# A mixture-of-experts kernel: each token's row is stored once in SBUF and carries both experts' data, and SyncE's copies of the normalized rows are taken out

## The reference

```python
x = x + elu(softmax(mask(leaky(e_src + e_dst))) @ Wh)      # of layernorm(x), Wh = layernorm(x) @ W
n = layernorm(x)
scores, idx = top_k(n @ Wg.T + bg, 2)                       # 2 of 8 experts
p = softmax(scores)                                         # p1 = 1/(1+exp(gap)), p2 = exp(gap)*p1
for e in range(8):
    y = relu(n @ W1[e].T + b1[e]) @ W2[e].T + b2[e]         # 128 -> 512 -> 128
    out = out + combine[..., e] * y                         # combine is p1, p2 or 0
x = x + out
```

## Time and profile before

| | |
|---|---|
| median of 3 runs | 451.71 us (451.34 to 453.06) |
| profiled execution, its span | 546.0 us (one execution; no other time of it is given) |
| engine busy, share of the span | TensorE 81%, VectorE 66%, ScalarE 58%, GpSimd 53% |
| attention steps, 60 to 246 us | TensorE 126.93 us busy, GpSimd 90.72 |
| steady expert blocks, 320 to 480 us | TensorE 159.91 us busy |
| SyncE's 32 copies into rows | 256 KB each |

### The profile page before, as it was taken

One profiled execution on the slowest core, in us unless ns is written; L12 is line 12 of the kernel. 1 busy time (PEld: TensorE's weight loads), 2 busy tenths in 40 slices (PEclk: granted clock), 3 DMA queues, 4 the chain that ended last, 5 costly groups with the idle time before them and its releaser, 6 DMA issues.

```text
span 546.0 us, 9056 instructions
## 1 busy us (share of the span) xinstructions
PE 443.0 (81%) x2246; PEld 330.6 (61%) x2246; DVE 362.3 (66%) x1410; ACT 318.7 (58%) x760; POOL 288.2 (53%) x292
## 2 busy tenths in 40 slices
PE   7796777665686776657998499999999999998990
PEld 3564555554464554545765388777778787886740
DVE  6576576566566664656786278678777777767754
ACT  2675466454555665547475397777777776757700
POOL 1206554444565544355467456655566565664662
PEclk8988887787888877777799799999999999999996
DMA  6982221122222211323324123332332323247789
GB/s 189 316 335 79 77 68 59 46 69 74 78 73 79 73 57 43 88 78 117 88 72 154 57 63 87 103 98 74 92 102 82 99 77 97 77 144 226 233 258 333
DMA packets 56291, 63.03 MB, mean 115 GB/s; under 512 B 7744, under 2 KB 40896, under 8 KB 56000
## 3 DMA queue, kind: packets, MB, share of 16 engines
q1 hardware_dynamic: 35728, 33.28, 20.6%
q0 software_dynamic: 9344, 20.10, 11.0%
q10 hardware_dynamic: 11184, 9.26, 5.6%
HBM read 27.28 MB, written 26.94 MB: 99 GB/s over the span
## 4 chain that ended last, share of the span: by engine, by line
PE 57%; another core or an unknown queue 13%; ACT 11%; issue 8%; DVE 6%; DMA 2%; SPq 2%; ACTq 1%; DVEq 0%; POOL 0%; POOLq 0%
PE bank L1438 6%; PE bank L1422 6%; PE bank L1435 6%; PE bank L1426 5%; PE bank L1436 5%; PE bank L1423 5%; PE bank L1323 5%; PE bank L1382 4%; ACT prob L595 4%; PE bank L1384 3%; PE bank L1304 2%; PE bank L1414 2%; PE bank L1406 2%; ACT xn L635 1%
## 5 line engine op out<-in xcount | busy, mean ns | idle before, releaser
L508 POOL DMA_INDIRECT expert_slots<-rows,slot_i x128 | 126.7, 990 | 132.4 <-DVE slot_i L872 94.7
L1323 PE MATMUL bank<-wh,prob_t 128*128 128x128 f32 x128 | 29.2, 400 | 51.4 <-ACT prob_t L603 45.1
L1435 PE MATMUL bank<-hh,w_hi 128*128 128x512 f32 x144 | 62.2, 432 | 5.7 <-DVE hh L1136 3.1
L700 ACT ACTIVATE yb<-bank,b_sb 128x512 f32<-128x512 f32 x36 | 24.8, 690 | 66.4 <-PE bank L1438 43.1
L1422 PE MATMUL bank<-xh,w_hi 128*128 128x512 f32 x144 | 60.6, 421 | 0.8 <-ACT xh L685 0.8
L1438 PE MATMUL bank<-hl,w_hi 128*128 128x512 f32 x144 | 59.6, 414 | 0.1
L1423 PE MATMUL bank<-xh,w_lo 128*128 128x512 f32 x144 | 58.6, 407 | 0.0
L1436 PE MATMUL bank<-hh,w_lo 128*128 128x512 f32 x144 | 58.4, 406 | 0.0
L1323 PEld LDWEIGHTS bank<-wh,prob_t 128*128 128x128 f32 x128 | 25.0, 291 | 55.0 <-ACT prob_t L603 47.9
L1426 PE MATMUL bank<-xl,w_hi 128*128 128x512 f32 x144 | 58.3, 405 | 0.0
L524 POOL DMA_INDIRECT moe_rows<-hrelu,ysi x40 | 41.4, 1035 | 30.5 <-issue 15.1
(11 more groups left out here) (166 smaller groups left out, 1108.8 us busy)
## 6 DMA issues: line engine op xcount, KB each, us to landing
rows<-xn SPq DMA_DIRECT2D x32, 256.0 KB
xs<-expert_slots SPq DMA_DIRECT2D x27, 260.0 KB
x_all<-x SPq DMA_DIRECT2D x16, 256.0 KB, 3.8
w_raw<-w_t SPq DMA_DIRECT2D x2, 2048.0 KB, 13.6
w_raw<-moe_rows SPq DMA_DIRECT2D x16, 256.0 KB, 4.1
out<-x_all ACTq DMA_DIRECT2D x16, 256.0 KB
xs<-expert_slots ACTq DMA_DIRECT2D x11, 260.0 KB
w_hi<-moe_rows SPq DMA_DIRECT2D x9, 256.0 KB, 4.6
```

Of the source, the lines that this page charges most:

```text
L508: nc.gpsimd.indirect_dma_start(out=slots, out_offset=bass.IndirectOffsetOnAxis(ap=slot_i[q][:, k * SUB + j:k * SUB + j + 1], axis=0), in_= ...
L700: nc.scalar.activation(yb[:, :], ps_y[:, :], ACT.Identity, bias=b2_sb[:, e:e + 1]).then_inc(yb_ok, 1)
L1323: last = nc.tensor.matmul(tiles(ps_av)[:, j, :], prob_t[:, j, :], wh[:, j, :], start=True, stop=True)
L1435: nc.tensor.matmul(ps_y[:, :], w2_hi[:, e, c, :], hh[:, c, :], start=c == 0, stop=False)
```

## The change

A token's row is now stored in SBUF once, in a ring of three buffers `rows[n]` (`RING`, group mod 3). ScalarE's second norm writes the features there directly, TensorE turns them from there, and GpSimd's eight DMAs of a group send the same four rows twice. SyncE's copies and the buffers `xn2` are gone. A row has 133 numbers: 128 features; `PICK`, two numbers, the difference of the first choice's weight and output number against the second's; `SECOND`, two numbers, the second choice's own; and `TOP`, the number of the expert that was chosen first. TOP is written by a new ScalarE copy (`top_rows`) behind the second norm, and GpSimd waits for it (`top_row_ok`) and for `xn2_ok` in place of `rowx_ok`. When a block is loaded, `keep_meta` picks: (TOP equals this block's expert) x PICK + SECOND. The block's expert comes from a table `expert_of` of 72 entries that VectorE computes once, from the block bounds and 72 new columns of constants. Output numbers are kept as float32.

```diff
-WEIGHT, ID = D, D + 1
-ROW = D + 2
+PICK, SECOND, TOP = D, D + 2, D + 4
+ROW = D + 5
+RING = 3
...
-        xn2 = [sb(f"xn2_{q}", [P, SUB, D]) for q in range(2)]
-        rows = [sb(f"rows{q}", [P, 2, SUB, ROW]) for q in range(2)]
+        rows = [sb(f"rows{n}", [P, SUB, ROW]) for n in range(RING)]
...
-                for k in range(2):
-                    sp.dma_start(rows[q][:, k, :, 0:D], xn2[q][:, :, :]).then_inc(rowx_ok, 16)
...
+            rows_sent(sp, SURE_GROUPS)
             load_block(sp, sure_row(0), 0)
...
                     pool.wait_ge(slot_ok, gr + 1)
-                    pool.wait_ge(rowx_ok, 32 * (gr + 1))
...
+                    pool.wait_ge(xn2_ok, SUB * (gr + 1))
+                    pool.wait_ge(top_row_ok, gr + 1)
...
-                                in_=rows[q][:, k, j, :], in_offset=None).then_inc(rows_out[q], 16)
+                                in_=rows[gr % RING][:, j, :], in_offset=None).then_inc(rows_out[gr % RING], 16)
...
+            def top_rows(gl):
+
+                act.wait_ge(topf_ok, gl + 1)
+                nc.scalar.copy(rows[gl % RING][:, :, TOP], top_f[:, 0, :]).then_inc(top_row_ok, 1)
...
-                if later(gx - 1):
-                    act.wait_ge(rowx_ok, 32 * (gx - 1))
+                if gx >= RING:
+                    act.wait_ge(rows_out[gx % RING], 16 * 2 * SUB * (gx // RING))
...
+            def weight_gap(gl):
+
+                dve.wait_ge(p2_ok, gl + 1)
+                nc.vector.tensor_tensor(rows[gl % RING][:, :, PICK], first_p[:, :], rows[gl % RING][:, :, SECOND], ALU.subtract)
...
-                nc.vector.tensor_copy(meta[:, bass.ds(i & (META - 1), 1), :, :].rearrange("p n t k -> p (n t) k"),
-                                      xs[:, :, WEIGHT:ROW]).then_inc(meta_ok, 1)
+                if not isinstance(i, int) or i > 0:
+                    dve.wait_ge(meta_ok, i + FIRST)
+                nc.vector.scalar_tensor_tensor(picked[:, :, :], xs[:, :, TOP:ROW].to_broadcast([P, SUB, 2]),
+                                               expert_of[:, bass.ds(i, 1)], xs[:, :, PICK:SECOND], ALU.is_equal, ALU.mult
+                                               ).then_inc(picked_ok, 1)
+                dve.wait_ge(picked_ok, i + 1)
+                nc.vector.tensor_tensor(meta[:, bass.ds(i & (META - 1), 1), :, :].rearrange("p n t k -> p (n t) k"),
+                                        picked[:, :, :], xs[:, :, SECOND:TOP], ALU.add).then_inc(meta_ok, 1)
...
+            nc.vector.tensor_tensor(reached[:, :, :], cst[:, C_BLOCK:C_END][:, :, None].to_broadcast([P, BLOCK_NOS, E]),
+                                    until_f[:, None, :].to_broadcast([P, BLOCK_NOS, E]), ALU.is_ge).then_inc(late_ok, 1)
+            dve.wait_ge(late_ok, 1)
+            nc.vector.tensor_reduce(expert_of[:, SURE_BLOCKS:], reached[:, SURE_BLOCKS:, :], AX, ALU.add).then_inc(late_ok, 1)
```

More of the change, by code:

```diff
@@ L44 @@
 STAGES = 5
+BLOCK_NOS = 72
 MASKED = -1e30
@@ L59 @@
 C_FULL = C_PAD + SUB
-C_END = C_FULL + FULL
+C_BLOCK = C_FULL + FULL
+C_END = C_BLOCK + BLOCK_NOS
 def shape_constants(np):
@@ L335, in gnn_moe_kernel @@
         x_in = [sem(f"x_in{n}") for n in range(LOADS)]
-        rows_out = [sem(f"rows_out{q}") for q in range(2)]
+        rows_out = [sem(f"rows_out{n}") for n in range(RING)]
         scattered = [sem(f"scattered{b}") for b in range(BUFS)]
@@ L340, in tiles, with rows_sent @@
             return ap[:, :].rearrange("p (t j) -> p t j", t=SUB)
+        def rows_sent(eng, groups):
+            for n in range(RING):
+                eng.wait_ge(rows_out[n], 16 * 2 * SUB * len(range(n, groups, RING)))
         def later(n):
@@ L422, in _ @@
             sp.dma_start(b2_sb[:, :], b2_t).then_inc(c_b2, 16)
[L424 to L434, removed]
-                for k in range(2):
-                    sp.dma_start(rows[q][:, k, :, 0:D], xn2[q][:, :, :]).then_inc(rowx_ok, 16)
[L438 to L443, removed]
+            rows_sent(sp, SURE_GROUPS)
             load_block(sp, sure_row(0), 0)
-            pass_on(SURE_GROUPS // 2 + 1, 1)
-            for q in range(2):
-                pass_on(GROUPS // 2 - 1, q)
             sp.wait_ge(table_ok, 1)
             bounds = [SURE_BLOCKS]
-            for q in range(2):
-                sp.wait_ge(rows_out[q], 16 * 2 * SUB * (GROUPS // 2))
+            rows_sent(sp, GROUPS)
             n = sp.value_load(count_i[0:1, E - 1:E], min_val=0, max_val=TOKENS)
@@ L672, in step @@
                 if gx is not None:
-                    second_norm(gx, q)
+                    second_norm(gx)
+                if gl is not None:
+                    top_rows(gl)
                 if g0 is not None:
@@ L712, in drain @@
                 elu_exp(last)
-                second_norm(last - 1, 0)
-                act.wait_ge(rows_out[0], 16 * 2 * SUB * (SURE_GROUPS // 2 + 1))
-                act.wait_ge(rows_out[1], 16 * 2 * SUB * (SURE_GROUPS // 2))
+                second_norm(last - 1)
+                top_rows(last - 2)
+                rows_sent(act, SURE_GROUPS)
                 load_block(act, sure_row(1), 1)
@@ L727, in drain @@
                 load_block(act, sure_row(2), 2)
-                second_norm(last, 1)
+                top_rows(last - 1)
+                second_norm(last)
                 turned_norm(last)
@@ L733, in drain @@
                 gap_exp(last)
+                top_rows(last)
                 hidden(1, 0, 2)
@@ L868, in write_slots @@
                 dve.wait_ge(slotp_ok, gr + 1)
-                if later(m - 2):
-                    dve.wait_ge(rows_out[q], 16 * 2 * SUB * (m - 2))
+                if gr >= 2:
+                    dve.wait_ge(rows_out[(gr - 2) % RING], 16 * 2 * SUB * ((gr - 2) // RING + 1))
                 with nc.allow_low_precision(reason="one term of a sum is a slot's number, the others are zero"):
@@ L1091, in step @@
                 if gl is not None:
-                    row_ids(gl, q)
+                    weight_gap(gl)
+                    row_ids(gl)
                 if isinstance(t, int) and t + 1 < len(BATCHES):
@@ L1192, in drain @@
                 gap_sum(last - 1)
-                first_weight(last - 1, q, m)
-                second_weight(last - 1, q)
-                row_ids(last - 1, q)
+                first_weight(last - 1)
+                second_weight(last - 1)
+                weight_gap(last - 1)
+                row_ids(last - 1)
                 halve(0, 2)
@@ L1213, in drain @@
                 weigh(0, 0, 0)
-                first_weight(last, 1 - q, (t + 1) // 2)
-                second_weight(last, 1 - q)
-                row_ids(last, 1 - q)
+                first_weight(last)
+                second_weight(last)
+                weight_gap(last)
+                row_ids(last)
                 write_slots(last, q, (t + 1) // 2)
@@ L1337, in rank, with norm_turns @@
                 last.then_inc(rank_ps, 1)
-            def norm_turns(gx, q):
+            def norm_turns(gx):
                 for j in range(SUB):
                     pe.wait_ge(xn2_ok, SUB * gx + (j + 1))
-                    last = nc.tensor.transpose(tiles(ps_t3)[:, j, :], xn2[q][:, j, :], ident)
+                    last = nc.tensor.transpose(tiles(ps_t3)[:, j, :], rows[gx % RING][:, j, 0:D], ident)
                 last.then_inc(xn2_ps, 1)
@@ L1463, in drain @@
                 pe.wait_ge(xn2_t_ok, last - 1)
-                norm_turns(last - 1, 0)
+                norm_turns(last - 1)
                 hidden(0, 0, 2)
@@ L1473, in drain @@
                 result(0, 0, 1)
-                norm_turns(last, 1)
+                norm_turns(last)
                 result(0, 0, 2)
```

71 lines of the change are left out of this document (38 added, 33 removed).

## The result

| | kernel before | changed kernel |
|---|---|---|
| median | 451.52 us (451.13 to 453.06, 4 runs) | 456.33 us (455.80 to 457.55, 4 runs) |
| ratio | 1 | 1.0114, 95% interval 1.0086 to 1.0143 |
| profiled span | 546.0 us | 454.7 us |

The changed kernel is 4.8 us (1.1%) slower. The forecast was 453.5, with 446 to 458 as the range: the sign and the range held, but the sum of 1.75 us was too small by a factor of 2.7. The median also lies above the 451.5 to 455.5 that the prediction gave to its own case D, near the times of the rivals B (457.2) and C (457.0).

What follows compares the result with a forecast made beforehand. TensorE was read as busiest (81%) and full in the expert blocks; in the attention steps a ring of work, no engine near full. Terms 0.3 + 1.0 + 0.3 + 0.15 = 1.75 us slower gave 453.5 us; range 446 to 458.

Steps and rivals of the forecast that it cites:

- case D: Whole kernel: the forecast itself, 451.5 to 455.5 us; chance 0.44.
- Rival B: Attention steps: GpSimd's start, 3.7 us later per group, is passed on; 457.2 us at most; chance 0.18.
- Rival C: Expert blocks: keep_meta costs in most blocks, half of 36, 4.5 us instead of 1.0; 457.0 us; chance 0.14.
- drain: Between attention and experts: three of the new ScalarE copies fall there, 0.1 each, 0.3 us.
- I take four such places: Expert blocks: keep_meta's second operation, some 0.25 us, shows in four places; 1.0 us, bounds 0 and 9.0.
- Together 3.0 us against 1.86 of idleness plus 0.9 of TensorE's lead: VectorE behind block 3: the table's 1.6 us plus 1.4 already there, mostly hidden; 0.3 us exposed, bounds 0 and 1.6.
- It cannot be in the measured time to that extent: Attention steps: the profiled stalls after SyncE's copies are mostly absent from runs; 94.3 us belong to the profiled execution alone.
- I take nothing: Attention steps: the copies' stalls in the measured time, between nothing and some 25 us, are put at 0.
- if the copies cause the stalls: Sign in the new profile: span falls to some 470 to 500 us, prob_t no longer waiting for an unknown releaser.
- 10.0 us a step, an estimate: Attention steps: unprofiled length of one of 11.7 steps, after taking 69.5 us of waits off 186 us.
- GpSimd's 10.2 us is a floor: Attention steps: GpSimd's eight scattered stores, 10.2 us a group, limit the step even if all stalls are removed.
- Rival A: Attention steps: part of the stalls is real and 6 us go, so the kernel is faster, 447.5 us; chance 0.24.

Runs made afterwards that it cites:

- e3: Kernel before with keep_meta as two dependent copies in place of one in each block; 453.49 us, ratio 1.0025.
- e7: Changed kernel with keep_meta's sum moved behind hl of chunk 0 and a smaller, later table over 42 blocks; 452.68 us, ratio 1.0023.
- e9: Changed kernel with only keep_meta's sum moved behind hl of chunk 0, table as it was; 453.17 us, ratio 1.0077.
- e5: Kernel before with the table of experts alone added, including its 72 columns of constants; 451.43 us, ratio 0.9999.
- e1: Changed kernel with ScalarE's copy of the expert number placed right behind the exponential of the gap, so GpSimd starts earlier; 456.03 us, ratio 1.0095.
- e4: Kernel before with only the step's additions: ScalarE's copy, GpSimd's wait for it, one more VectorE subtraction; 451.19 us, ratio 1.0011.
- c0: Kernel before, unchanged, profiled a second time; span 451.0 us, and the run took 452.85 us.
- e6: Kernel before with 7 + 3 filler matmuls, results unused, in the drain; 448.76 us, ratio 0.9938.
- e2: Changed kernel with 7 + 3 filler matmuls, results unused, in the drain; 452.52 us, ratio 1.0051.
- e8: Kernel before with one unused tile of 32 bytes per partition ahead of xs, no instruction changed; 449.20 us, ratio 0.9982.

## Why the prediction held, and which terms were mis-sized

The forecast's mechanism was right in the main: the removed copies were hidden, and most of the rise that can be assigned is VectorE's new work in the expert blocks. Its size was not: every term that showed was put too low, and the time stayed in the range because the range was wide. The terms, beside what they measured:

| term | put at | measured |
|---|---|---|
| keep_meta | 4 places x 0.25 = 1.0 | 8 places x 0.24 = 1.9 (e3; gone in e7, e9) |
| table | 0.3 | 1.0 in the changed kernel, 0.65 in e5 |
| drain | 0.3 | up to 0.9, from profiles that scatter by 0.6; 0.1 with fillers |
| steps, ring, GpSimd, SyncE | 0 | 0.2 (e1 and e4: none that can be told) |
| constants | 0.15 | not seen; the fourth z copy starts at 40.4 to 43.5 us, whatever the kernel |
| addresses of tiles | not thought of | steady blocks 6.43 for 6.46: -0.6 |

These add up to +3.4 us. The runs say +4.8 (3.9 to 6.5) for the changed kernel and +4.3 (3.0 to 5.6) for e1. So 0.9 to 1.7 us (by the ratio 5.1 for the changed kernel) are not assigned, and up to 0.9 more if the drain is no part of the loss.

- **"I take four such places".** This is the step that failed most. The price of a place was right (0.25 against 0.24 in the mean); the count was an estimate. The earlier trace rows were taken in a steady block, and the places that matter were within the reach of the same trace: every change of expert, eight of them.
- **"Together 3.0 us against 1.86 of idleness plus 0.9 of TensorE's lead".** The 1.86 us come from a steady block too. Behind block 3 VectorE also makes the low halves of the weights and has no idle time. The duration of 1.6 us was nearly right (0.78 + 0.72), the cover was not.
- **The drain.** The three ScalarE copies were priced by their length. The time that can be won in the drain lies elsewhere, in short gaps on TensorE after which its clock is at half, and both kernels have them. That the new operations lengthen these gaps is not shown.
- **"It cannot be in the measured time to that extent" and "I take nothing".** Right: 94.3 us belonged to that one execution. The first followed from the two times; the second was a choice between 0 and 25 us, made with numbers of the odd profile, and there luck helped. What I said would show the cause was worthless, though. The new profile's span did fall below 500 us with prob_t waiting no longer, just as "if the copies cause the stalls" demanded, and the copies did not cause them: c0 has them and spans 451.0. A comparison with one profile of each kernel could not have told this.
- **10.0 us a step, an estimate** from the distorted profile, was 10.2. GpSimd's own figure held too: in the steps its stores start 1.26 us apart without a pause, 10.1 us a group. But "GpSimd's 10.2 us is a floor" names an engine that is as full as the step is long, not the one that sets it: between 60 and 160 us no engine waits for GpSimd in either kernel, the chain does not touch it, and e1, which shifts its stores by 2.5 to 3 us, changes nothing, while VectorE is busy 93%.
- **Rival A** (faster) needed real stalls and had none. **Rival B** named 3.7 us; the shift was 0.8 to 1.3, and starting 2.5 to 3 us earlier gains nothing (e1). **Rival C**, "in most blocks", gave 457.0, near the result, but by the wrong account: its 18 blocks are 8, TensorE is busy 99.6% in the blocks (159.36 of 160 us), and the table and what is not assigned make up the rest.

## What to carry to other kernels

A price per operation is the easy half; the count of places where it shows is the other. Go through the profile for each kind of place (first block of a loop, change of weights, drain), and there look at who runs right behind the engine that gets more work: an engine's long wait just ahead is no cover, if what it waits for also starts the one behind it. When a profiled span is far from the runs' times, profile the same kernel again before explaining anything by that profile.

## What the runs showed of the hardware

- One execution of the unchanged kernel spanned 546.0 us at a mean granted clock of 0.894, another 451.0 at 0.971.
- In both kernels TensorE's clock is at half for 7 to 10 us on end in the drain, after idle gaps of 1.58 and 0.63 us (changed kernel; 1.41 and 0.63 in c0); ten matmuls whose result is unused take 2.3 to 3.5 us off the time (e6, e2).
- Two dependent small VectorE operations cost 0.24 us more than one, of which the second is itself 0.17. The Trainium skill (VectorE: DVE Perf Modes, "The DRAIN you can't avoid") says that eight copies took the same 13.88 us with a semaphore after each and with one only after the last. No run here takes the semaphore away between the same two operations, so that is not tested. In the changed kernel the second operation starts 0.26 us after the first and waits for it, and in e7 an independent operation follows the first after 0.13. The waits of the changed kernel list seven of 0.2 us (us in total, times, longest):

```profile
DVE meta L1126 <- DVE picked L1122: 1.6, 7, 0.2
```

- Matmuls of 128x512 in f32r follow each other at 228 to 229 ns in e4, e5 and e8, and at 232 to 234 in c0, e7 and the changed kernel, with the same TensorE instructions in c0, e4, e5 and e8. In the fast ones the tile xh and the weights lie alike modulo 64 bytes, in the slow ones 32 bytes apart. The addresses are worked out from the order and the sizes of the tiles in each kernel. The matmuls on hh show no such clear rule (229 to 238 ns), so the rule is a guess.
